# Two-run values, split turn banks and earlier row gathers in a two-layer block kernel

## The reference

```python
# layer 0, mixture of experts (E = 8, TOP_K = 2, H = 1024, CAPACITY = 512)
out = out + combine[:, e][:, None] * (gelu(xf @ W1[e] + b1[e]) @ W2[e] + b2[e])     # for each e
x = x + out
# layer 1, conditioning: attention with 16 heads of 16 features
scores = einsum('bhqd,bhkd->bhqk', Q, K) / sqrt(16)
s_scores = ...                      # 32 listed keys a query: the kernel adds log(count) of each key as a bias
sparse_out = softmax(s_scores) @ V
out = where(use_sparse, sparse_out, dense_out) @ Wo.T + bo
```

## Time and profile before

| | us |
|---|---|
| median of 3 runs (lowest, highest) | 2055.51 (2054.39, 2059.71) |
| the profiled execution's own time | 2059.76 |
| its span | 2058.0 |
| PE busy in the span | 1886.6 (92%) |
| DVE busy | 1131.7 (55%) |
| ACT busy | 941.0 (46%) |
| POOL busy | 451.6 (22%) |
| largest shares of the chain that ended last | PE 71%, DVE 19%, issue 3%, DMA 2%, ACT 2% |

### The profile page before, as it was taken

How to read it: one execution, slowest core, us unless ns; L and a number is a source line. 1 busy time by engine, 2 the same in 40 slices (tenths; PEclk the granted TensorE clock), 3 DMA queues, 4 the chain that set the end, 5 groups by cost and what they waited for, 6 DMA issues and landing times.

```text
span 2058.0 us, 37788 instructions
## 1 busy us (share of the span) xinstructions
PE 1886.6 (92%) x15665; PEld 1374.2 (67%) x15665; DVE 1131.7 (55%) x2325; ACT 941.0 (46%) x1647; POOL 451.6 (22%) x504
## 2 busy tenths in 40 slices
PE   5988898986988949999999999999999999999997
PEld 3366885773656645666776677766787778777776
DVE  4474542025232126888887888864555554445544
ACT  2213023102232304778887888863455544445522
POOL 1353110004221033212121212103232222223313
PEclk9779568997999979999999999999999999999999
DMA  4000021201332339521110301000000000000001
GB/s 130 0 1 1 1 68 43 85 21 62 97 129 82 103 123 192 114 38 36 26 31 20 106 20 38 20 2 21 1 2 1 2 1 1 1 27 2 1 0 42
DMA packets 85198, 86.97 MB, mean 42 GB/s; under 512 B 34659, under 2 KB 70947, under 8 KB 84899
## 3 DMA queue, kind: packets, MB, share of 16 engines
q1 hardware_dynamic: 79154, 73.81, 13.0%
q0 software_dynamic: 3072, 8.39, 1.4%
q10 hardware_dynamic: 2800, 2.34, 0.4%
HBM read 65.65 MB, written 18.87 MB: 41 GB/s over the span
## 4 chain that ended last, share of the span: by engine, by line
PE 71%; DVE 19%; issue 3%; DMA 2%; ACT 2%; POOL 1%; SPq 0%; DVEq 0%; POOLq 0%
PE PS L1046 8%; DVE arena L1709 7%; PE PS L1038 7%; PE PS L1859 6%; PE PS L1904 5%; PE PS L1920 5%; PE PS L1542 5%; PE PS L1555 5%; PE PS L1894 4%; DVE arena L1714 4%; PE PS L1534 3%; PE PS L1864 3%; PE PS L525 2%; PE PS L478 1%; PE PS L1927 1%
## 5 line engine op out<-in xcount | busy, mean ns | idle before, releaser
L1709 DVE CUSTOM_DVE_ANT_0 arena<-PS,arena 128x1024 f32<-128x1024 f32 x256 | 312.7, 1222 | 73.5 <-PE PS L1534 58.9
L1542 PE MATMUL PS<-arena 128*128 128x128 f32 x2048 | 282.1, 275 | 20.2 <-DVE arena L1714 20.1
L1542 PEld LDWEIGHTS PS<-arena 128*128 128x128 f32 x2048 | 241.4, 142 | 87.2 <-DVE arena L1714 34.9
L1633 ACT ACTIVATE arena<-arena 128x1024 f32<-128x1024 f32 x256 | 295.0, 1152 | 10.0 <-DVE arena L1709 10.0
L2107 POOL TENSOR_SCALAR arena<-arena 128x448 f32<-128x448 f32 (+1 forms) x256 | 152.8, 613 | 394.3 <-DVE arena L2035 393.1
L2006 ACT ACTIVATE arena<-arena 128x449 f32<-128x449 f32 (+1 forms) x256 | 161.5, 632 | 141.3 <-DVE arena L2044 141.3
L1629 ACT COPY arena<-PS 128x512 f32<-128x512 f32 x256 | 150.3, 587 | 101.1 <-PE PS L1542 93.4
L1714 DVE COPY arena<-PS 128x512 f32<-128x512 f32 x256 | 175.8, 687 | 1.2 <-PE PS L1542 1.2
L1038 PE MATMUL PS<-arena 128*128 128x512 f32 x384 | 169.8, 600 | 6.6 <-ACT arena L1137 6.6
L1046 PE MATMUL PS<-arena 128*128 128x256 f32 x768 | 172.0, 385 | 0.0
L2044 DVE CUSTOM_DVE_ANT_0 arena<-PS,arena 128x448 f32<-128x448 f32 (+1 forms) x256 | 136.7, 588 | 59.9 <-PE PS L1895 58.8
(11 more groups left out here) (280 smaller groups left out, 2679.5 us busy)
## 6 DMA issues: line engine op xcount, KB each, us to landing
arena<-in_L_ffn_W SPq DMA_DIRECT2D x16, 1024.0 KB, 6.5
arena<-prior SPq DMA_DIRECT2D x16, 512.0 KB, 3.8
parts<-arena SPq DMA_DIRECT2D x24, 256.0 KB, 4.8
arena<-parts SPq DMA_DIRECT2D x96, 64.0 KB, 2.9
arena<-parts SPq DMA_DIRECT2D x48, 128.0 KB, 9.2
ye<-arena SPq DMA_DIRECT2D x8, 512.0 KB, 3.5
prior<-arena SPq DMA_DIRECT2D x4, 1024.0 KB, 9.0
arena<-in_xT SPq DMA_DIRECT2D x2, 1024.0 KB, 8.1
```

The lines of the kernel that those rows point to most:

```text
L1542: h = e.transpose(PS[:, i, P * j:P * j + P], Sb[z % 3][:, 512 * g + P * j:512 * g + P * j + P], ident)
L1633: e.activation(Sb[z % 3], Sb[z % 3], ACT.Exp, bias=mr[:, z % 4:z % 4 + 1], scale=-1.0).then_inc(s_exp, 1)
L1709: e.tensor_tensor_reduce(Sb[z % 3], ps, Ab[m % 2], 1.0, 3e38, ALU.add, ALU.min, mr[:, z % 4:z % 4 + 1]).then_inc(s_ttr, 1)
```

## The change

1. *Last expert.* In turn 7 PE forms three of expert 7's eight hidden groups, then expert 6's outputs, then the other five hidden groups. `result` waits for each hidden group by itself rather than for the last.
2. *Rows by expert.* Outputs of experts 0 to 6 are stored twice, in `ye` and in `ya` (both on SP's queue), those of expert 7 in `yl` alone, from where a DMA copies them to `ya` later. The tiles of sequence 0 are combined in 24 gathers: 16 from `ye` with expert 7's weight set to zero, which need experts 0 to 6 only, then 8 from `yl`, one a tile. DVE adds the first 8 in turn 7, 2 more between expert 7's two output groups and 14 behind them. Sequence 1 has its 16 gathers from `ya`, once the copy has landed; DVE adds two after each of sequence 0's projections. SP issues the copy and three weight loads after 20 additions. DVE has 10 more small instructions in the routing for the second set of weights and indices.
3. *Logarithms.* ACT takes the logarithm of turns 3, 4 and 5 behind the turn's GELUs and count copies, that of turn 7 in front of them as before.
4. *Preparation.* A sequence's transposes wait for four tiles at a time; for sequence 0 two projections stand between the second and the third transpose.
5. *Loop.* The values of four heads go in two runs of 4 chunks per four steps (in the steps z with z modulo 4 equal to 3 and 1), ahead of the step's transposes. Group 0 has banks 4 and 5 (with `gather` and `close`), group 1 has bank 6 to itself. In every sixth step ACT copies group 0 too. Sequence 0's closing groups are spread over 38 steps.

The diff, cut to its core:

```diff
--- before.py
+++ after.py
@@ -851,7 +851,9 @@
-    Ye = nc.dram_tensor("ye", (E * CAP, D), F32, kind="Internal").ap()
+    Ye = nc.dram_tensor("ye", ((E - 1) * CAP, D), F32, kind="Internal").ap()
+    Yl = nc.dram_tensor("yl", (CAP, D), F32, kind="Internal").ap()
+    Ya = nc.dram_tensor("ya", (E * CAP, D), F32, kind="Internal").ap()
@@ -934,17 +940,24 @@
+    EARLY = 3
     for q in range(E + 1):
...
             for f in range(8):
+                if q == E - 1 and f == EARLY:
+                    plan_out("eo", q - 1)
                 ring.plan(("eh", q, f), "act")
...
-        if q:
+        if q and q != E - 1:
             plan_out("eo", q - 1)
 
+    ROWS = [(t, k) for t in range(TB_) for k in range(2)] + [(t, None) for t in range(TB_)] + [(t, k) for t in range(TB_, NT) for k in range(2)]
@@ -959,11 +972,20 @@
+    def store_last(e, w):
+        w.wait_ge(s_yl, 16)
+        e.dma_start(Ya[CAP * (E - 1):CAP * E, :], Yl).then_inc(s_ye[(E - 1) % 2], 16)
...
-    def combined(w, b):
-        w.wait_ge(s_comb, 2 * TB_ * (b + 1))
+    def combined(w, b, t=TB_):
+        w.wait_ge(s_comb, 3 * TB_ + 2 * t if b else 2 * TB_ + t)
@@ -1011,7 +1033,12 @@
                 w.wait_ge(*ring.emptied(("eo", q - 1, 2)))
-                e.dma_start(Ye[CAP * (q - 1):CAP * q, :].rearrange("(t p) c -> p t c", p=P), ye[(q - 1) % 2]).then_inc(s_ye[(q - 1) % 2], 16)
+                y = ye[(q - 1) % 2]
+                if q == E:
+                    e.dma_start(Yl.rearrange("(t p) c -> p t c", p=P), y).then_inc(s_yl, 16)
+                else:
+                    e.dma_start(Ye[CAP * (q - 1):CAP * q, :].rearrange("(t p) c -> p t c", p=P), y).then_inc(s_ye[(q - 1) % 2], 16)
+                    e.dma_start(Ya[CAP * (q - 1):CAP * q, :].rearrange("(t p) c -> p t c", p=P), y).then_inc(s_ye[(q - 1) % 2], 16)
@@ -1112,18 +1139,25 @@
-                hidden("eh", q, xgT[q % 2], 0, exw[q % 2][0])
+                hidden("eh", q, xgT[q % 2], 0, exw[q % 2][0], range(EARLY if q == E - 1 else 8))
...
                 result("eo", q - 1, hb[(q - 1) % 2], exw[(q - 1) % 2][1])
+            if q == E - 1:
+                hidden("eh", q, xgT[q % 2], 0, exw[q % 2][0], range(EARLY, 8))
@@ -1135,9 +1169,8 @@
-            if q in FORMS:
-                w.wait_ge(s_form, 2 * FORMS[q] + 2)
-                e.activation(lbw, lbw, ACT.Ln).then_inc(s_log, 1)
+            if q == E - 1:
+                logs(q)
             for f in range(8):
...
+            if q < E - 1:
+                logs(q)
@@ -1285,34 +1331,38 @@
-                result("eo", q - 1, b2e[:, D * (q - 1):D * q], ye[(q - 1) % 2])
+                for t in (0, 2):
+                    result("eo", q - 1, b2e[:, D * (q - 1):D * q], ye[(q - 1) % 2], (t,))
+                    if q == E and not t:
+                        for m in range(8, 10):
+                            add_rows(e, w, m)
             if q in FORMS:
                 differ(FORMS[q])
-        K.combine_dve(e, w)
+            if q == E - 1:
+                for m in range(8):
+                    add_rows(e, w, m)
+        for m in range(10, 3 * TB_):
+            add_rows(e, w, m)
...
+    def fetch_rows(e, w, m):
+        t, k = ROWS[m]
+        if m >= 8:
+            w.wait_ge(s_comb, m - 7)
+        src, at_ = (Yl, G7[:, t:t + 1]) if k is None else (Ya if t >= TB_ else Ye, GI[:, k, t:t + 1])
+        e.indirect_dma_start(gt[m % 8], None, src[:, :], bass.IndirectOffsetOnAxis(ap=at_.bitcast(U32), axis=0)).then_inc(s_g[m % 8], 16)
@@ -1330,11 +1380,16 @@
-        for t in range(NT):
-            fetch_rows(e, w, t)
+        w.wait_ge(*ring.filled(("count", 15)))
+        w.wait_ge(s_ye[0], 32 * E // 2)
+        w.wait_ge(s_ye[1], 32 * (E // 2 - 1))
+        for m, (t, k) in enumerate(ROWS):
+            if k is None:
+                w.wait_ge(s_yl, 16)
+            elif t >= TB_:
+                w.wait_ge(s_ye[1], 32 * E // 2 - 16)
+            fetch_rows(e, w, m)
@@ -1376,8 +1431,10 @@
-    ring = Ring(K.sem("e_filled"), {"act": K.sem("e_emptied_act"), "dve": K.sem("e_emptied_dve")}, [4, 5, 6])
+    ring = Ring(K.sem("e_filled"), {"act": K.sem("e_emptied_act"), "dve": K.sem("e_emptied_dve")}, [4, 5])
+    ring1 = Ring(K.sem("e_filled1"), {"act": K.sem("e_emptied1_act")}, [6])
@@ -1391,9 +1448,11 @@
+            return turns[:2] + first + turns[2:] + rest + [("V", b, j) for j in range(4)]
+        return part(0, (0, 1), [("P", 0, 0, 0), ("P", 0, 1, 0)]) + part(1, (2, 3), [])
@@ -1409,26 +1468,31 @@
+    CLOSE = {135 + 4 * k if k < 4 else 131 + 6 * k: (0, k) for k in range(8)}
+    CLOSE.update({263 + k: (1, k) for k in range(8)})
+    def turned_by(z, g):
+        return "act" if g or z % 6 == 5 else "dve"
...
-        if z >= 5 and (z - 5) // 4 < NZ // 4 and (z - 5) % 4:
-            return (z - 5) // 4 * 4, ((0, 1, 2), (3, 4, 5), (6, 7))[(z - 5) % 4 - 1]
+        for lag, ks in ((7, range(4)), (9, range(4, 8))):
+            if z >= lag and (z - lag) % 4 == 0 and z - lag < NZ:
+                return z - lag, ks
@@ -1465,7 +1529,11 @@
-        for dst, n in ((Wq4, "Wq"), (Wk4, "Wk"), (Wv4, "Wv"), (Wo4, "Wo")):
+        e.dma_start(Wq4, kmaj(a["L1_cond_Wq"])).then_inc(s_w0, 16)
+        K.combined(w, 0, 4)
+        K.store_last(e, w)
+        for dst, n in ((Wk4, "Wk"), (Wv4, "Wv"), (Wo4, "Wo")):
@@ -1582,10 +1656,10 @@
                 scores(z)
+            if summed(z):
+                values(*summed(z))
             if 2 <= z < NZ + 2:
                 turn(z - 2)
-            if summed(z):
-                values(*summed(z))
@@ -1693,15 +1770,17 @@
-                if s[1] == 0 and s[0] != "T" and added:
-                    K.add_rows(e, w, added.pop(0))
+                if s[0] == "V" or (s[0] == "P" and s[1] < 2):
+                    for m in added[:2]:
+                        K.add_rows(e, w, m)
+                    del added[:2]
```

134 lines of the change are left out of this document (75 added, 59 removed).

## The result

The kernel before takes 2054.95 us (median of 4 runs, 2054.32 to 2059.71), the changed one 2031.46 us (4 runs, 2028.64 to 2033.23): the ratio is 0.9874 [0.9856, 0.9892], faster by 1.3%. (Ratios here are estimates over all runs of both kernels and can differ by a tenth of a per cent from the quotient of the medians, 0.9886 in this case, 23.5 us.) The forecast was 1998.5 in 1989 to 2024: the sign is right, the size is not, and the time lies outside the range. The profiled execution took 2031.93 us.

What follows compares the result with a forecast made beforehand. The prediction took PE's queue as the bound, gains coming from stretches where PE waits: loop -45, seam -15, second stores +3, together -57 from 2059.76 to 2002.8, less 4.25 for the median: 1998.5 us, range 1989 to 2024.

Steps and rivals of the forecast that it cites:

- The loop: Phase E's loop: four steps fall from 8.24 to 7.48 us, 48.6 us less 4 given back, so -45 us.
- 0.12 and 0.10 for the runs and 0.54 for DVE's copy: Loop, per four steps: two runs for three save 0.12, one entry fewer 0.10, no wait for DVE's copy 0.54 us.
- the prediction's own sign of being wrong in the main thing: Loop: the prediction is wrong in the main thing if the period of four steps stays above 8 us.
- The entry from scores: Loop on PE: switching from scores to values costs 0.10 us, at most 0.16; the upper end costs 8 us.
- Rival A: Loop: tight bank 6 and DVE bind, 19 us lost, 27 with the dearer entry, some 2018 to 2026; chance 0.24.
- Rival B: Loop: values ahead of transposes delay group 0's copy and DVE's next bias; slower if over 0.49 us a pair; chance 0.04.
- The seam: Between phases D and E: PE's 26.89 us idle stretch shrinks as gathers start earlier, -15 us.
- rival C: Seam: copy and gathers late under neighbouring loads, 9 us instead of 15, 2005 us; chance given only as part of the range.
- The second stores: Turns 4 and 5: the second store ahead of the prior's quarter on SP costs 1.5 us in two turns, +3 us.
- logarithms: Turns 4 and 5: moving them behind the GELUs gains nothing, since DVE's third one-hot matrix still releases the last count.
- The closing groups: Loop: the same instructions elsewhere, so spreading them gains or costs nothing.
- The 4 us for bank 6 in the sixth steps: Loop: ACT copying both groups makes a copy late, 0.1 us for each of 43 steps, 4 us given back.

Runs made afterwards that it cites:

- e4: Kernel before with only the banks split (group 0 in 4 and 5, group 1 in 6), three values runs behind the transposes: 2038.19 us, ratio 0.9847.
- e5: Changed kernel with PE's two values runs behind the step's transposes instead of ahead: 2012.79 us, ratio 0.9742.
- e1: Changed kernel with ACT's copy of finished head outputs (OT copy) put ahead of the step's exponential: 2023.18 us, ratio 0.9775.
- e2: Changed kernel with DVE copying group 0 in every step, no sixth-step copy on ACT: 2035.99 us, ratio 0.985.
- e3: Kernel before with only the values changed, to two runs of four chunks ahead of the transposes, three banks still shared: 2039.73 us, ratio 0.9857.
- e0: Changed kernel unaltered, run again in the second set on another chip: 2035.18 us, ratio 0.985.
- e6: Changed kernel with DVE adding no row of sequence 1 behind the first two projections: 2036.08 us, ratio 0.9856.
- e8: Changed kernel with three weights, value bias and first prior rows loaded ahead of the copy to `ya` on SP: 2029.25 us, ratio 0.9877.
- e9: Changed kernel with the second stores of experts 2, 3 and 4 behind the prior's quarter on SP's queue: 2029.85 us, ratio 0.9864.
- e10: Changed kernel with the logarithms of turns 3, 4 and 5 ahead of the GELUs again: 2030.66 us, ratio 0.987.

## Why the prediction was wrong

**The loop** (-45 forecast, -24.6 measured with the 1.9 us behind it) is the step that failed. The terms were right: 0.12 and 0.10 for the runs and 0.54 for DVE's copy. e4 has the 0.54 alone (7.71), e5 has all three (7.51). Nor did the prediction's own sign of being wrong in the main thing, a period above 8 us, appear; it was set too wide. What failed is that moving the values ahead of the transposes was given no price but the entry:

| four steps | us |
|---|---|
| forecast, and e5 | 7.48, 7.51 |
| e1: values ahead, transposes restarted behind them | 7.60 |
| e2: and the OT copy behind the exponential | 7.87 |
| the change, where a sixth step is among the four | 7.92 |

The 0.27 us for the OT copy is the large part: 64 x 0.27 = 17 us. It could be had from the code and the earlier trace rows: a values run that begins a new group of four heads waits for `s_e_ot`, and ACT has an exponential of 1.15 us ahead of that copy. The prediction followed ACT's copy of group 1 to hundredths of a microsecond and did not ask what else ACT releases. The restart behind values is 0.05 to 0.06, twice in four steps; e1 against e5 has 0.09 for it, some 6 us. With the 0.03 between e5 and the forecast that is 0.39 in four steps, 25 us, less 2 us that the sixth steps did not cost (next paragraphs): 23 against the 20.4 by which the loop missed. Most of the rest is the stop of PE told in the last section, which was 1.9 us worse before than after. The entry from scores, taken as 0.10 with 0.16 as the upper end, was well placed: scores to values is 0.53 from start to start where scores to transposes is 0.44, so 0.09.

**Adding the two edits** was a mistake of the same kind that had no consequence in the sum, but one in the reading: with the values ahead, e3 has lost the wait for DVE's copy already without split banks (8.24 - 0.12 - 0.10 - 0.54 + 0.27 + 0.11 = 7.86; from one values run to the next but one it is 7.84 in its trace). Only one edit can be credited with it. Of the two, the split banks without the new place are the better half by the trace (7.71); the times alone (0.9847 and 0.9857) don't tell them apart.

**Rival A** named the tight places as bank 6 and DVE. The wait for bank 6 is there only around the sixth steps, 0.05 us each (7.92 against 7.87, and e2 has none); the sign that the prediction gave for A, over 0.1 us at the second transposes, did not appear, and DVE is not late. So A did not happen, though the time came out near its end. The rule of the Trainium skill on copies out of PSUM (TensorEngine Tiling (Array Packing), Performance Considerations) was set aside because ACT idles ahead of its copy. It bears on this case after all, not as a matter of throughput but of order: ACT is busy for 446 of 532 us and still the copy is late for its taker, by its place in the order. Rival B, which was to end slower by the same move of the values, had the right place and the wrong victim: its point from which it decides was 0.49 us a pair, and the trace has 0.22 ((7.92 - 7.48) / 2).

On what the Trainium skill (TensorEngine Tiling (Array Packing), Key Properties) says of draining: the trace has 0.09 on entering a run of values and 0.05 behind leaving it, both less than the 0.16 by which a transpose's modelled end lies beyond the next start. A change of mode costs something in both directions; no run here shows a full drain.

**The seam** (-15 forecast, -8.9 measured in the first profiles) went as rival C said, and there at its price of 9; on the chips of the first two sets it gave 12, by the stops told under e0, which neither had a term for. The hit of the 9 is in part luck: C named the late gathers, and half of the loss is the clock. The early part is right: expert 7's outputs, the gathers from `ye` (first forecast for 725, 725.6 without the lag), the copy to `ya` (5 us forecast, 764.36 - 759.34 = 5.0), the first transposes. What failed is the sentence "its next two transposes need the eighth, at 758.6, when PE is still at the two projections": the eighth gather lands 8.1 us after its issue, not 3.45. And no term stood for the clock, 4.3 us, which the kernel before did not pay at this place. e6 and e8 shift the waits about and gain nothing.

**The second stores** (+3 forecast, +2.9) were right in their sum and cause (e9), though not as 1.5 us in each of two turns: it was 1.5, 0.7 and 0.6 in three. The **logarithms** (0, e10) were right with their mechanism. **The closing groups** cost 9.2 us in sequence 0's end now and 9.6 before: nothing, as forecast. The 4 us for bank 6 in the sixth steps were too many: e2 finds 2 at most.

The range failed with the loop: its far end, 2024, was built from known tight places with a price each, and the one that bound wasn't among them.
